# First loads cut into five parts from one row block on, A rows loaded in front of the odd weights, last output stored in three pieces

## The chip, the cores and the metric

The kernel runs on one core of a Trainium2 chip. The metric is the device time of one launch in microseconds (us), and the median of several runs is compared. Lower is better.

## The reference, cut to what matters

Two residual steps on x of shape (128, 64, 1024). The first adds a linear layer with a low-rank adapter chosen per batch element; the second adds a long convolution whose filter is built from a state-space model.

```python
x = x + (einsum('bsd,od->bso', x, W) + bias + einsum('bsr,bor->bso', einsum('bsd,brd->bsr', x, A[ids]), B[ids]))
K = 2 * real(einsum('hn,hnl->hl', Ct, exp(dtA[:, :, None] * arange(1024))))
y = irfft(rfft(x, 2048) * rfft(K, 2048))[..., :1024] + x * D[:, None]
x = x + where(arange(1024) < length, y, 0)
```

Everything is float32. Each product on TensorE is made of three: an operand is split into a rounded part (hi) and what is left (lo), and hi*hi + hi*lo + lo*hi are summed.

## The kernel before, in words

The 128 batch elements are 16 groups of G = 8. One group's x is a tile of NT = 8 row blocks (k = 0 to 7) of 128 rows and N = 512 columns (64 heads by 8 elements). In stage 1 each group goes through the linear layer; output tiles of even number have one set of weights (`w_even`, blocks of `w_pair`) and those of odd number another (`w_odd`, in `v_raw`, `v_hi`, `v_lo`). For most of the work a seven-product scheme with sums of weight blocks is used, but group 0's even tiles are computed plainly: `first_tiles` runs over k, and for each k does QT = 2 output tiles with 3 matmuls each; `plain_tile(2)`, `adapters_down(0)` (x times the A rows), `plain_tile(3)`, `plain_adapters` and the odd products follow. Stage 2 goes over the 64 heads: convolution by blocks, states, and `apply`, which writes the sum into `out_sb` where the mask allows.

All work is ordered by hand, one program per engine, with semaphores between them. SP issues every DMA in the order written. ScalarE (ACT, helper `copy`, L687) writes every hi, VectorE (DVE, `minus_hi`, L1106) every lo, TensorE (PE) multiplies.

At the start SP issues, for `part` 0 to 3, `load_w0(part)` (2 row blocks of first even weights, 256 KB) and `load_x0(part)` (2 row blocks of x, 512 KB), each with a semaphore of its own; after part 0 the adapter ids; then `load_w(0)`, `load_w(1)`, three blocks of odd weights (`load_v`, 512 KB each), a wait for the ids, eight reads of an id into a register (L437), eight A rows (`load_a`, 64 KB each), the bias, eight B rows (`load_b`) and the last block of odd weights.

DVE adds the identity to two diagonal blocks of these weights (`keep_residual`, L1114): this puts the residual x into the product. Part 0 and part 1 have one such block each, and ACT's `split_w0(part)` waits for it. ACT and DVE both go part by part: the weights first, then the two row blocks of x (`split_x`). In `first_tiles` PE waits at every second k for the part's weights (`c_w0lo`) and at every k for `c_xlo`. Until then PE multiplies the identity by itself (`spin`, L1900, SPINS = 14), begun as soon as the identity is there.

After the x parts DVE does `t1(0)`, `split_w(0)`, `keep_residual_22`, `split_w(1)`, the odd weights' `weight_sum_1` (which waits for its three blocks), `split_a(0)`, `weight_sums_3_2`, `split_b(0)`, then `keep_own(0)` and `split_h(0)`, on which `plain_adapters(0)` waits.

At the end, the last head's output is written by two calls of `apply`, one for each half (`par`, a bank of 512 columns), and each half is stored when `c_last` says so:

```python
for par in range(2):
    sp.wait_ge(c_last, par + 1)
    sp.dma_start(out[heads - 1, :, par * BANK:(par + 1) * BANK], ...).then_inc(st_last, 16)
```

## Time and profile before

| what | value |
|---|---|
| median of 3 runs | 1073.74 us (1071.79 to 1074.54) |
| the profiled execution, whole time | 1078.09 us |
| its span in the trace | 1076.4 us |
| TensorE clock granted over the span | 1.00 of full speed (2.4 GHz) |
| PE busy | 1064.2 us (99%) |
| DVE busy | 848.9 us (79%) |
| ACT busy | 716.7 us (67%) |
| DMA queues | 284.62 MB, mean 264 GB/s |

Busy time counts an engine's instructions alone; PE's matmuls overlap and their ends are modelled, so small waits of PE are best read from the starts of its matmuls. A row of the timeline merges instructions of one form that follow each other, with their count, and gives the idle time in front of them and what ended it in brackets.

### The profile page before, as it was taken

Reading aid. Unit: us, or ns where it says so; the run is one execution under the profiler, and the core shown is the slowest. Engines: PE = TensorE matmul, PEld = TensorE weight load, DVE = VectorE, ACT = ScalarE, POOL = GpSimd, SP = SyncE. Lnnn points to the kernel's source line nnn. Section 1 sums busy time; section 2 is a strip of 40 time slices with the busy share of each in tenths; the row PEclk is TensorE's granted clock in tenths of the full one; section 3 lists DMA queues with packets and bytes.
Section 4 is the critical chain, followed back from the end, with each engine's and each line's share of the span. In section 5 each row is a group of like instructions: output and inputs, shape, how many; then the busy total and the mean of one; then the engine's idle time right before and its main releaser. Section 6 shows DMA issues by size and latency. Waiting matters only on the chain.

```text
span 1076.4 us, 21569 instructions
## 1 busy us (share of the span) xinstructions
PE 1064.2 (99%) x8088; PEld 1030.1 (96%) x8088; DVE 848.9 (79%) x1263; ACT 716.7 (67%) x1260; POOL 28.7 (3%) x79
## 2 busy tenths in 40 slices
PE   9999999999999999999999999999999999999998
PEld 8999999999999999999999999999989999999997
DVE  7898886869797696978777696877488888888886
ACT  5755546755747566565647566465498888888885
POOL 0000000000000000000000000000010000000000
PEclk9999999999999999999999999999999999999999
DMA  8586858689786957878785967868798979788873
GB/s 307 193 285 223 273 165 287 199 286 298 243 284 203 289 201 274 245 268 281 228 295 182 302 217 260 284 238 272 251 345 309 337 293 326 305 315 330 287 272 125
DMA packets 162586, 284.62 MB, mean 264 GB/s; under 512 B 10739, under 2 KB 125620, under 8 KB 149044
## 3 DMA queue, kind: packets, MB, share of 16 engines
q1 hardware_dynamic: 162484, 283.26, 76.8%
q8 instruction: 64, 1.05, 0.4%
q14 instruction: 38, 0.31, 0.1%
HBM read 193.96 MB, written 89.26 MB: 263 GB/s over the span
## 4 chain that ended last, share of the span: by engine, by line
PE 59%; SPq 12%; DVE 8%; DMA 8%; ACT 7%; issue 5%; DVEq 0%; ACTq 0%; POOL 0%; POOLq 0%
PE acc L1974 25%; PE acc L1814 16%; PE acc L1820 8%; DMA a_raw<-lora_a 5%; DMA x_scratch<-x_sb 3%; SPq L437 3%; SPq L487 3%; PE acc L2009 3%; DVE x_lo L1106 3%; SPq L441 2%; PE acc L1742 2%; SPq L445 2%; PE acc L1752 2%; PE acc L1786 2%; DVE x_sb L1265 1%
## 5 line engine op out<-in xcount | busy, mean ns | idle before, releaser
L1974 PE MATMUL acc<-u_hi,f_hi 128*128 128x512 f32 (+1 forms) x320 | 128.8, 403 | 0.0
L1814 PE MATMUL acc<-t_hi,v_hi 128*128 128x256 f32 x512 | 123.4, 280 | 5.2 <-ACT x_sb L687 5.2
L1814 PE MATMUL acc<-t_hi,w_pair 128*128 128x256 f32 x960 | 122.6, 280 | 0.8 <-ACT t_hi L687 0.8
L1814 PE MATMUL acc<-t_hi,v_lo 128*128 128x256 f32 x512 | 123.0, 279 | 0.0
L687 ACT ACTIVATE acc<-acc 128x512 f32<-128x512 f32 x93 | 54.0, 580 | 102.9 <-PE acc L1820 102.8
L1974 PE MATMUL acc<-u_lo,f_hi 128*128 128x512 f32 (+1 forms) x320 | 118.3, 370 | 0.0
L1974 PE MATMUL acc<-u_hi,f_lo 128*128 128x512 f32 (+1 forms) x320 | 118.2, 369 | 0.0
L1814 PEld LDWEIGHTS acc<-t_hi,w_pair 128*128 128x128 f32 x960 | 116.8, 188 | 1.2 <-issue 1.1
L1814 PEld LDWEIGHTS acc<-t_hi,v_hi 128*128 128x128 f32 x512 | 96.2, 188 | 6.3 <-ACT x_sb L687 6.3
L1106 DVE TENSOR_TENSOR t_lo<-t_raw,t_hi 128x1024 fp32r<-128x1024 f32 x64 | 78.2, 1222 | 28.0 <-ACT t_hi L687 27.2
L1814 PEld LDWEIGHTS acc<-t_hi,v_lo 128*128 128x128 f32 x512 | 96.2, 188 | 0.0
L1814 PE MATMUL acc<-x_hi,w_pair 128*128 128x256 f32 x720 | 92.9, 281 | 0.5 <-DVE w_pair L1106 0.5
L1814 PE MATMUL acc<-x_hi,v_hi 128*128 128x256 f32 x384 | 92.5, 280 | 0.2 <-ACT acc L687 0.2
L1814 PE MATMUL acc<-x_hi,v_lo 128*128 128x256 f32 x384 | 92.3, 279 | 0.0
L690 ACT ACTIVATE x_sb<-acc,bias_sb 128x256 f32<-128x256 f32 (+1 forms) x128 | 54.6, 482 | 53.9 <-PE acc L1786 52.6
L687 ACT ACTIVATE t_hi<-t_raw 128x1024 fp32r<-128x1024 f32 x64 | 67.7, 1057 | 33.6 <-DVE t_raw L1223 30.3
L1814 PEld LDWEIGHTS acc<-x_hi,w_pair 128*128 128x128 f32 x720 | 87.7, 188 | 1.3 <-issue 0.7
L1664 DVE COPY_PREDICATED out_sb<-mask,acc 128x1024 f32<-128x1024 uint8 (+1 forms) x65 | 84.8, 1306 | 2.4 <-PE acc L1974 2.4
L1106 DVE TENSOR_TENSOR s_lo<-s_raw,s_hi 128x256 fp32r<-128x256 f32 (+1 forms) x128 | 45.1, 353 | 47.9 <-ACT s_hi L687 47.8
L1106 DVE TENSOR_TENSOR x_lo<-x_raw,x_hi 128x512 fp32r<-128x512 f32 x128 | 80.1, 686 | 1.1 <-ACT x_hi L687 0.3
L1106 DVE TENSOR_TENSOR u_lo<-u_raw,u_hi 128x1024 fp32r<-128x1024 f32 (+1 forms) x64 | 77.5, 1211 | 1.3 <-ACT u_hi L687 1.3
L687 ACT ACTIVATE s_raw<-acc 128x128 f32<-128x128 f32 x192 | 51.9, 270 | 32.6 <-PE acc L2009 21.6
(205 smaller groups left out, 2677.2 us busy)
## 6 DMA issues: line engine op xcount, KB each, us to landing
w_pair<-weight_scratch SPq DMA_DIRECT2D x71, 1024.0 KB, 7.9
x_scratch<-x_sb SPq DMA_DIRECT2D x32, 1024.0 KB, 6.6
out<-out_sb SPq DMA_DIRECT2D x63, 512.0 KB, 4.5
x_raw<-x_t SPq DMA_DIRECT2D x15, 2048.0 KB, 12.1
u_raw<-x_scratch SPq DMA_DIRECT2D x14, 2048.0 KB, 11.9
wq_raw<-state_scratch SPq DMA_DIRECT2D x16, 1024.0 KB, 7.7
a_raw<-lora_a SPq DMA_DIRECT2D x128, 64.0 KB, 6.1
b_raw<-lora_b SPq DMA_DIRECT2D x128, 64.0 KB, 2.2
```

The lines of the kernel that those rows point to most:

```text
L437: row = sp.value_load(ids_sb[0:1, b:b + 1], min_val=0, max_val=n_adapters - 1)
L441: sp.dma_start(a_raw[:, i, :, :].rearrange("p t r -> p (t r)"), lora_a[row, :, :].rearrange("a p n -> (a p) n")).then_inc(ld_a, 16)
L445: sp.dma_start(b_raw[i * rank:(i + 1) * rank, :, :].rearrange("p t n -> p (t n)"), lora_b[row, :, :].rearrange("a r n -> (a r) n")).then_i ...
L487: sp.dma_start(r32(w_pair[:, n % 2, :, :, :, :]).rearrange("p s k i n -> p (s k i n)"), ws_d[STREAM.index(j)].rearrange("p s k n -> p (s k ...
L687: return act.activation(dst, src, ACT.Copy)
L690: return act.activation(dst, src, ACT.Identity, bias=bias_sb[:, tile:tile + 1])
L1106: return dve.tensor_tensor(dst, src, r32(hi), ALU.subtract)
L1664: return dve.copy_predicated(out_sb[h % OUT_BUFS][:, pars, :, :].rearrange("p k g n -> p (k g n)"), mask[:, pars, :, :, :].rearrange("p k ...
L1814: pe.matmul(by_row(bank_part(bank, i)), w[:, k, i, :], hi[:, k, :, :], start=opens and i == 0 and k == 0 and s == 0, stop=False, skip_grou ...
L1820: mm = pe.matmul(by_row(bank_part(bank, i)), w_hi[:, k, i, :], lo[:, k, :, :], start=False, stop=False, skip_group_check=True)
L1974: mm = pe.matmul(bank, w, m, start=first and i == 0, stop=last and i == 2, skip_group_check=onto_closed)
L2009: pe.matmul(state_cols(h, i + 1), rot[h % 2][:, :, :].rearrange("p k n -> p (k n)"), s_raw[h % 2][:, :, i, :], start=False, stop=True, ski ...
```

## The change

The first loads are cut at row blocks 1, 2, 4, 6, so into five parts of 1, 1, 2, 2 and 2 row blocks. The first part keeps one semaphore for w and one for x; in each later part w and x share one semaphore, and whoever needs either waits until both have landed (32). The ids are loaded after part 1, not 0. In the first part ACT and DVE split x in front of the weights. The A rows are loaded in front of the three blocks of odd weights, and DVE splits them in front of `weight_sum_1`. The second diagonal block lies in part 2 (row block 2). The last head's second half is written and stored in two pieces.

```diff
     ld_x = sem("ld_x")
-    X0_PARTS = 4
-    ld_x0 = [sem(f"ld_x0_{i}") for i in range(X0_PARTS)]
-    W0_PARTS = 4
-    ld_w0 = [sem(f"ld_w0_{i}") for i in range(W0_PARTS)]
+    FIRST_PARTS = ((0, 1), (1, 2), (2, 4), (4, 6), (6, 8))
+    ld_first_x, ld_first_w = sem("ld_first_x"), sem("ld_first_w")
+    ld_first = [sem(f"ld_first_{i}") for i in range(1, len(FIRST_PARTS))]
     ld_w = [sem(f"ld_w{i}") for i in range(2)]
     ld_ws = [sem(f"ld_ws{i}") for i in range(2)]
...
     EVEN, ODD, BOTH = slice(0, 1), slice(1, 2), slice(0, 2)
+    LAST_PIECES = ((0, slice(0, n_groups)), (1, slice(0, n_groups // 2)), (1, slice(n_groups // 2, n_groups)))
     def u_loaded(q):
...
         return UNIT_PLACES.index((g, place)) if (g, place) in UNIT_PLACES else None
+
+    def first_loaded(part, alone):
+        return alone if part == 0 else ld_first[part - 1]
+
+    def first_rows(part):
+        k0, k1 = FIRST_PARTS[part]
+        return k0 // HALF, k0 % HALF, k0 % HALF + k1 - k0
+
+    def part_of(k):
+        return [k0 <= k < k1 for k0, k1 in FIRST_PARTS].index(True)
     def taps_group(c):
...
             def load_x0(part):
-                w = NT // X0_PARTS
-                sp.dma_start(x_raw[:, part * w:(part + 1) * w, :].rearrange("p t n -> p (t n)"),
-                             x_t[0, :, part * w * N:(part + 1) * w * N]).then_inc(ld_x0[part], 16)
+                k0, k1 = FIRST_PARTS[part]
+                sp.dma_start(x_raw[:, k0:k1, :].rearrange("p t n -> p (t n)"),
+                             x_t[0, :, k0 * N:k1 * N]).then_inc(first_loaded(part, ld_first_x), 16)
             def adapter_of(g, i):
...
             def load_w0(part):
-                c, k = divmod(part * 2, HALF)
+                c, k0, k1 = first_rows(part)
                 w = QT * P
-                sp.dma_start(w_raw[:, c, 1, k:k + 2, :, :].rearrange("p k i n -> p (k i n)"),
-                             w_even[0, c, :, k * w:(k + 2) * w]).then_inc(ld_w0[part], 16)
+                sp.dma_start(w_raw[:, c, 1, k0:k1, :, :].rearrange("p k i n -> p (k i n)"),
+                             w_even[0, c, :, k0 * w:k1 * w]).then_inc(first_loaded(part, ld_first_w), 16)
             def load_w(c):
...
-            for part in range(X0_PARTS):
+            for part in range(len(FIRST_PARTS)):
                 load_w0(part)
                 load_x0(part)
-                if part == 0:
+                if part == 1:
                     sp.dma_start(ids_sb[:, :], ids).then_inc(ld_ids, 16)
             load_w(0)
             load_w(1)
-            load_v(v_raw[:, A11, :, :, :], 0, 0, ld_v11)
-            load_v(v_raw[:, A22, :, :, :], 1, 1, ld_v22)
-            load_v(a21_raw[:, :, :, :], 1, 0, ld_v21)
             sp.wait_ge(ld_ids, 16)
             rows = [adapter_of(0, i) for i in range(G)]
             for i, row in enumerate(rows):
                 load_a(i, row)
+            load_v(v_raw[:, A11, :, :, :], 0, 0, ld_v11)
+            load_v(v_raw[:, A22, :, :, :], 1, 1, ld_v22)
+            load_v(a21_raw[:, :, :, :], 1, 0, ld_v21)
             sp.dma_start(bias_sb[:, :], bias_t).then_inc(ld_bias, 16)
             for i, row in enumerate(rows):
...
                     if q + U_BUFS < quads:
                         load_u(q + U_BUFS)
-            for par in range(2):
-                sp.wait_ge(c_last, par + 1)
-                sp.dma_start(out[heads - 1, :, par * BANK:(par + 1) * BANK],
-                             out_sb[(heads - 1) % OUT_BUFS][:, par, :, :].rearrange("p g n -> p (g n)"))\
+            for i, (par, gs) in enumerate(LAST_PIECES):
+                sp.wait_ge(c_last, i + 1)
+                sp.dma_start(out[heads - 1, :, par * BANK + gs.start * W8:par * BANK + gs.stop * W8],
+                             out_sb[(heads - 1) % OUT_BUFS][:, par, gs, :].rearrange("p g n -> p (g n)"))\
                   .then_inc(st_last, 16)
-            sp.wait_ge(st_last, 32)
+            sp.wait_ge(st_last, 16 * len(LAST_PIECES))
             for i in range(OUT_BUFS):
                 sp.wait_ge(st_out[i], 16 * len(range(i, heads - 1, OUT_BUFS)))
...
             def split_w0(part):
-                act.wait_ge(ld_w0[part], 16)
-                if part < 2:
-                    act.wait_ge(c_wid, part + 2)
-                c, k = divmod(part * 2, HALF)
-                copy(w_pair[:, c, 0, k:k + 2, :, :], w_raw[:, c, 1, k:k + 2, :, :]).then_inc(c_w0hi, 1)
+                if part == 0:
+                    act.wait_ge(ld_first_w, 16)
+                    act.wait_ge(c_wid, 2)
+                else:
+                    act.wait_ge(first_loaded(part, ld_first_w), 32)
+                if part == part_of(2):
+                    act.wait_ge(c_wid, 3)
+                c, k0, k1 = first_rows(part)
+                copy(w_pair[:, c, 0, k0:k1, :, :], w_raw[:, c, 1, k0:k1, :, :]).then_inc(c_w0hi, 1)
             def split_w(c):
...
             def split_x(g, t):
-                if g == 0:
-                    act.wait_ge(ld_x0[t * X0_PARTS // NT], 16)
+                if g == 0 and t == 0:
+                    act.wait_ge(ld_first_x, 16)
+                elif g == 0:
+                    act.wait_ge(first_loaded(part_of(t), ld_first_x), 32)
                 elif t == 0:
                     act.wait_ge(ld_x, 16 * g)
...
             act.wait_ge(c_zero, 1)
             copy(hh[0:heads, 0:1], zeros[:, 0:1])
-            for part in range(W0_PARTS):
+            for part, (k0, k1) in enumerate(FIRST_PARTS):
+                if part == 0:
+                    split_x(0, 0)
                 split_w0(part)
-                for t in range(part * NT // 4, (part + 1) * NT // 4):
+                for t in range(max(k0, 1), k1):
                     split_x(0, t)
             split_w(0)
...
                 return dve.tensor_tensor(ap, ap, ident, ALU.add)
-            def keep_residual(part):
-
-                dve.wait_ge(ld_w0[part], 16)
-                add_identity(w_raw[:, 0, 1, 2 * part, part, :]).then_inc(c_wid, 1)
-                dve.wait_ge(c_wid, part + 2)
+            def keep_residual(i):
+
+                if i == 0:
+                    dve.wait_ge(ld_first_w, 16)
+                else:
+                    dve.wait_ge(first_loaded(part_of(2 * i), ld_first_w), 32)
+                add_identity(w_raw[:, 0, 1, 2 * i, i, :]).then_inc(c_wid, 1)
+                dve.wait_ge(c_wid, i + 2)
             def keep_residual_22():
...
             def split_w0(part):
                 dve.wait_ge(c_w0hi, part + 1)
-                c, k = divmod(part * 2, HALF)
-                ks = slice(k, k + 2)
+                c, k0, k1 = first_rows(part)
+                ks = slice(k0, k1)
                 minus_hi(w_pair[:, c, 1, ks, :, :], w_raw[:, c, 1, ks, :, :], w_pair[:, c, 0, ks, :, :]).then_inc(c_w0lo, 1)
...
             dve.memset(zeros[:, :], 0.0).then_inc(c_zero, 1)
             make_identity()
-            for part in range(W0_PARTS):
-                if part < 2:
-                    keep_residual(part)
+            for part, (k0, k1) in enumerate(FIRST_PARTS):
+                for i in range(QT):
+                    if part == part_of(2 * i):
+                        keep_residual(i)
+                if part == 0:
+                    split_x(0, 0)
                 split_w0(part)
-                for t in range(part * NT // 4, (part + 1) * NT // 4):
+                for t in range(max(k0, 1), k1):
                     split_x(0, t)
             t1(0)
             keep_residual_22()
             split_w(1)
+            split_a(0)
             weight_sum_1()
-            split_a(0)
             weight_sums_3_2()
             split_b(0)
...
                 filter_step(g, 3)
+            def apply_piece(h, par, gs):
+
+                y = acc[:, y_bank(h) + par, gs.start * W8:gs.stop * W8]
+                return dve.copy_predicated(out_sb[h % OUT_BUFS][:, par, gs, :].rearrange("p g n -> p (g n)"),
+                                           mask[:, par, gs, :, :].rearrange("p g t b -> p (g t b)"), y)
+
             def apply(h, pars=slice(0, 2)):
...
             last = heads - 1
             state_low(last, 2, 3)
-            for par in range(2):
+            dve.wait_ge(c_x1c, heads)
+            for par, gs in LAST_PIECES:
                 dve.wait_ge(m_y, last + par + 1)
-                apply(last, slice(par, par + 1)).then_inc(c_last, 1)
+                apply_piece(last, par, gs).then_inc(c_last, 1)
...
             def first_tiles():
                 for k in range(NT):
-                    if k % 2 == 0:
-                        pe.wait_ge(c_w0lo, k // 2 + 1)
+                    if k == FIRST_PARTS[part_of(k)][0]:
+                        pe.wait_ge(c_w0lo, part_of(k) + 1)
                     pe.wait_ge(c_xlo, k + 1)
                     for i in range(QT):
```

## Rows read from the trace of the kernel before

**Rows 1.** The page, its first part: busy us, share and instructions of each engine.

```profile
PE 1064.2 (99%) x8088; PEld 1030.1 (96%) x8088; DVE 848.9 (79%) x1263; ACT 716.7 (67%) x1260; POOL 28.7 (3%) x79
```

**Rows 2.** The timeline of PE and its weight loads: start, us, what, count.

```profile
1.48 5.53 PE L1900 MATMUL acc<-rot 128*128 128x128 f32 x28 [1.48 <-DVE rot L1110]
6.76 0.48 PE L1752 MATMUL acc<-x_hi,w_pair 128*128 128x512 f32 x1
...
9.39 0.89 PE L1752 MATMUL acc<-x_hi,w_pair 128*128 128x512 f32 x2
...
23.51 0.39 PE L1742 MATMUL acc<-x_hi,a_st 128*128 128x256 f32 x1
...
32.86 0.28 PE L1778 MATMUL acc<-hh,b_st 128*128 128x256 f32 x1
...
9.78 0.19 PEld L1752 LDWEIGHTS acc<-x_hi,w_pair 128*128 128x128 f32 x1 [0.42 <-issue]
```

**Rows 3.** The timeline of ACT.

```profile
4.37 0.63 ACT L687 ACTIVATE w_pair<-w_raw 128x512 fp32r<-128x512 f32 x1 [2.06 <-DVE w_raw L1114]
...
8.30 1.16 ACT L687 ACTIVATE x_hi<-x_raw 128x512 fp32r<-128x512 f32 x2 [0.28 <-DMA x_raw<-x_t]
...
21.43 1.16 ACT L687 ACTIVATE a_st<-a_raw 128x512 fp32r<-128x512 f32 x2 [3.17 <-DMA a_raw<-lora_a]
23.60 2.14 ACT L687 ACTIVATE b_st<-b_raw 64x1024 fp32r<-64x1024 f32 x2 [1.01 <-DMA b_raw<-lora_b]
```

**Rows 4.** The timeline of DVE.

```profile
3.98 0.29 DVE L1114 TENSOR_TENSOR w_raw<-w_raw,rot 128x128 f32<-128x128 f32 x1 [2.56 <-DMA w_raw<-w_even]
5.11 0.69 DVE L1106 TENSOR_TENSOR w_pair<-w_raw,w_pair 128x512 fp32r<-128x512 f32 x1 [0.83 <-ACT w_pair L687]
...
8.97 1.29 DVE L1106 TENSOR_TENSOR x_lo<-x_raw,x_hi 128x512 fp32r<-128x512 f32 x2
...
24.63 1.22 DVE L1147 TENSOR_TENSOR v_raw<-v_raw 128x1024 f32<-128x1024 f32 x1
25.88 2.47 DVE L1106 TENSOR_TENSOR b_st<-b_raw,b_st 64x1024 fp32r<-64x1024 f32 x2
28.39 0.68 DVE L1251 TENSOR_TENSOR h_own<-acc,h_own 64x512 f32<-64x512 f32 x1
```

**Rows 5.** The timeline of SP's queue.

```profile
2.49 0.43 SPq L432 DMA_DIRECT2D x_raw<-x_t  x1
...
12.62 3.97 SPq L441 DMA_DIRECT2D a_raw<-lora_a  x8
```

**Rows 6.** DMAs issued at 2.49, 21.5, 21.95, 1073.53: KB each, us to landing.

```profile
x_raw<-x_t SPq DMA_DIRECT2D x1, 512.0 KB, 5.8
...
b_raw<-lora_b SPq DMA_DIRECT2D x2, 64.0 KB, 2.0
...
v_raw<-w_odd SPq DMA_DIRECT2D x1, 512.0 KB, 3.9
...
out<-out_sb SPq DMA_DIRECT2D x1, 256.0 KB, 2.0
```

**Rows 7.** Stretches: busy us by engine, granted clock, DMA share, GB/s.

```profile
5.00:6.00 1.00, 1.00 (x7) 1.00 (x6) 0.89 (x2) 0.90 (x3) 0.00 (x0) 1.00 0.75 231
194.00:196.50 2.50, 1.16 (x9) 1.16 (x10) 1.09 (x3) 2.50 (x7) 0.00 (x0) 1.00 1.00 410
1074.00:1075.00 1.00, 0.00 (x0) 0.00 (x0) 0.00 (x0) 0.00 (x0) 0.00 (x0) 1.00 1.07 416
```

**Rows 8.** The timeline of DVE and SP at the end.

```profile
1072.17 0.73 DVE L1664 COPY_PREDICATED out_sb<-mask,acc 128x512 f32<-128x512 uint8 x1 [0.97 <-PE acc L1974]
...
1072.80 0.70 DVE L1664 COPY_PREDICATED out_sb<-mask,acc 128x512 f32<-128x512 uint8 x1
1072.93 0.33 SPq L676 DMA_DIRECT2D out<-out_sb  x1
...
1073.53 0.33 SPq L676 DMA_DIRECT2D out<-out_sb  x1
```


## The prediction

> **What bounds the kernel now.** The page's first part comes first: PE is busy for 1064.2 of 1076.4 us [rows 1], DVE for 848.9. So a change of loads can be worth only what PE waits at the start, and what stands between its last matmul and the end. The timeline of PE shows the start [rows 2]: the identity products (`spin`) begin at 1.48 and last till about 7.0, the first product of `first_tiles` starts at 6.76, the twelfth (the last of row blocks 0 and 1) at 9.39. Then PE waits once: by its pace the next would start at 9.62, but its weights are loaded at 9.78. The pace is 0.23 us a matmul, from (23.51 - 9.88) / 60, where 9.88 is that weight load and 0.10 more. After this it runs without a gap into `adapters_down` (23.51), `plain_tile(3)` and `plain_adapters` (32.86).
>
> What ended that wait is read from ACT and DVE [rows 3, 4]. ACT starts the hi of x's row block 2 at 8.30, when the DMA lands (issued at 2.49, landed 5.8 us later [rows 5, 6]); DVE's lo runs from 8.97 to about 9.62; PE has it at 9.78. So PE starts row block 2 1.49 us after its x has landed. The weights of that part were ready before: ACT's and DVE's work on them lies in the time in which x was still on its way.
>
> **The first parts.** Part 0 is half as large and x is split first, so its lo values can be there sooner than in the kernel before. It buys nothing: PE comes to `first_tiles` when the spins are over, at 6.76 as now, for nothing in the change starts or shortens them [rows 2]. Row block 1 is needed at 6.76 + 6 * 0.23 = 8.1; its bytes, with part 0's, are those of the old part 0, of which ACT split the weights at 4.37 and DVE at 5.11 [rows 3, 4]. Both are costed at zero, hidden by the spins. If that cover were gone, about 0.6 us could be saved at row block 0 (half of ACT's 0.63 and of DVE's 0.69), but PE would only wait longer at row block 2.
>
> **Row block 2.** Here lies the cost. Its x and w come with part 2, behind the same 1536 KB as before, and now share a semaphore. The identity for the second diagonal block (`keep_residual(1)`) thus waits for x as well, and behind it on DVE stand `split_w0(2)` and the x splits; on ACT `split_w0(2)` waits for both loads and for that identity, and x's hi stands behind it; PE waits for the last of these. From landing L the chain is: 0.05 to start, the identity 0.29, 0.10 to ACT, weights' hi 0.63, 0.11 to DVE (all from the rows at 3.98, 4.37 and 5.11 [rows 3, 4]), weights' lo 0.69, x's lo 0.65 (half of 1.29, with no wait, as its hi was made meanwhile), 0.16 to PE (9.62 to 9.78). Sum 2.68 us, where it was 1.49: 1.19 later.
>
> L itself was 2.49 + 5.8 = 8.29. The bytes ahead of it don't change, so I take 8.3. Bounds: x of part 2 is issued behind two DMAs more, at 0.45 each (0.43 and a gap [rows 5]), so if it keeps its 5.8 us it lands at 9.2 (cost 2.1). The stretch from 5 to 6 us moved 231 GB/s and others 410 [rows 7]; with that dip gone the 180 KB missing come 0.44 us sooner, L = 7.85 (cost 0.75). The rows of the two small parts are half as long, 1 KB for w; what that costs isn't in a row here, and I leave it inside these bounds. Taken: **+1.2 us**, PE idle from 9.62 to about 11.0.
>
> The rules for kernel authors in the Trainium skill's page "DMA: Bandwidth & Descriptors" speak against this part: they ask for 1 MiB or more in a DMA. By the page's fit of a fixed 2.0 us and bytes / 436 GB/s, an estimate, a lone 128 KB load would land 2.3 us after its issue and a 256 KB one 2.6; the trace's comparable time is that of a B row of 64 KB, 2.0 us [rows 6]. By either the small parts would be there long before the spins end, so neither changes the sum.
>
> Parts 3 and 4 have their shared semaphore too. DVE is free of part 2 at about 11.5; part 3 (768 KB more at 410 GB/s: landed at 10.2) then has its weights' lo and x's at 12.8, and PE wants it at 11.0 + 2.7 = 13.7. Part 4, 1.9 later again, is landed at 12.1, ready at 14.9 and wanted at 16.4. Nothing more is lost there. `plain_tile(2)` wants its second weights at about 21.8; DVE, 0.8 later than now, has them at 20.4.
>
> **A rows in front of the odd weights.** In the SP queue the three `load_v` go away from in front of the id reads (1.4 us) and two first loads come in (0.9), so A rows are issued from about 12.1, not 12.62 [rows 5], till 16.0. They no longer stand behind 1.5 MB: last issue 15.6 plus 2.0 to 5.0 gives 17.6 to 20.6, where ACT waited 3.17 us for them until 21.43 [rows 3]. But PE did not wait: `adapters_down` starts at 23.51 on its pace, and will be wanted at 24.7. Worth zero now; it would be worth something only to a PE that came sooner. What it costs is behind it: the odd weights are issued at 16.1 to 17.5 and everything after them in the queue (bias, B rows, the fourth odd block) 0.9 later. A lone 512 KB took 3.9 us [rows 6], further ones 1.3 each: the third lands at about 22.6. DVE then has three sums of 1.22 (22.7 to 26.3) and two lo of B of 1.22 (to 28.7) [rows 4]; B lands at 22.4 + 2.0 = 24.4 (ACT took it at 23.60). `keep_own` can begin at 28.7, where it now begins at 28.39. PE, 1.2 late, gives it its input at 29.6. So there are 0.9 us of cover and the cost is zero. With no delay of PE it would be 0.3; if the odd weights landed 2 us later than that, 1.1 on top of what is forecast.
>
> All that follows hangs on PE or on this DVE chain, both later by about the same; PE has no long wait to absorb it, as its 99% says [rows 1].
>
> **The end.** DVE copies the first half at 1072.17 (0.73) and the second at 1072.80 (0.70); the stores are issued at 1072.93 and 1073.53 [rows 8], and the second lands after 2.0 us [rows 6]. In three pieces the first is unchanged. A half copy costs about 0.4 (512 columns take 0.70), so the second store is issued at 1073.3 and the third, held by the queue's 0.37 per issue, at 1073.67: 0.14 after the old second. The DMA engines are saturated from 1074 to 1075 (share 1.07, 416 GB/s [rows 7]), so pieces that come sooner wait behind the first 256 KB and the last byte leaves when it did. Bounds: -0.2 (landing shrinks with a store of 128 KB: 0.33 less 0.14) to +0.3 (short rows are slower). Taken: **+0.1**.
>
> **Sum.** 1.2 + 0.1 = +1.3 us. Made on the profiled execution (1078.09 whole, 1076.4 span), which is 4.35 above the median of the runs; the difference is carried over to the median: 1073.74 + 1.3 = 1075.0.
>
> **Rivals.**
> 1. The loads come sooner and the wait shrinks. To break even at row block 2, L must be 7.1, 1.2 sooner; the most that can be had is the present wait, 0.26. Then about -0.2, 1073.5. For it: the dip to 231 GB/s. Against: the same bytes. 10%.
> 2. Landing is set by the issue, not by the bytes: L = 9.2, cost 2.1, with the end 1076.0. For it: the 5.8 us are longer than 512 KB needs; against: by the rates in [rows 7] the queue was full. 20%.
> 3. TensorE's clock falls. PE would idle 1.4 us just after its start. In the stretch from 194.0 to 196.5 PE was idle for 1.34 us and the granted clock stayed at 1.00, 2.4 GHz [rows 7]. Were it 1.2 GHz for a stretch after the wait, half of the stretch would be lost; with 1.3 already gone, 4 us of it make the kernel slower by over 0.3% (3.2 us), and over all 8.2 us of the rest of `first_tiles`, which would take 16.4, it is 1083.2. 4%. The Trainium skill, "TensorE: Matmul & The Clock Gate", its HAM clock gate part, has PE drop to half clock after idling; the stretch above bears no such drop out.
> 4. The odd weights or B come much later than reckoned, and DVE's chain sets `plain_adapters`: +2.4, 1076.1. 6%.
>
> The forecast itself has 60%, with 1074.3 to 1076.1 as its own range (cost 0.75 to 2.1, end -0.2 to +0.3). The medians of either kernel move too (the three runs span 2.8 us), so the range is 1072.5 to 1077.5. Within 0.3%, about what this measurement can tell from no change, lie the forecast and rivals 1, 2 and 4: 93%, less a little for both tails. Faster by more would need 3.2 us, and PE waits for less than that at the start: 2%. Slower: 5%, rival 3 and an unforeseen wait.
>
> **What would show it.** In the changed kernel's profile: spins and first product at 1.48 and 6.76 as before; one gap of PE at row block 2, its matmuls from about 11.0; in front of it on DVE the order identity, w lo, x lo, with the identity waiting for x's DMA at about 8.3; `adapters_down` at about 24.7 with A rows split by 21.7; `keep_own` at about 29.6; the last store issued 0.14 later after the last matmul. Wrong would be: row block 2 before 10, a wait of PE at `plain_adapters`, a clock below 1.00, or an end above 1077.5.

## The result

The changed kernel's median is 1076.49 us (1073.64 to 1079.22, 22 runs) against 1073.15 us for the kernel before (1071.31 to 1075.28, 22 runs beside it). The ratio is 1.0029, 95% interval 1.0021 to 1.0037: 3.1 us slower by the ratio, 3.3 by the medians. That is just inside the 0.3% that the prediction took as no change, and the loss is real, since the interval excludes 1. Forecast was +1.3 us. The predicted range of 1072.5 to 1077.5 held the time, but 2 us of the loss were not in the sum. The forecast's own narrower range (1074.3 to 1076.1) did not hold it. The wide one did with some luck: it starts from 1073.74, the median of three runs, and the median of 22 is 0.6 lower.

The profiled execution of the changed kernel took 1075.75 us, with a span of 1074.0. This is less than the 1078.09 of the kernel before, so spans of single executions say nothing here; the two are compared by the starts of the same work. What stands behind the first product of the odd tiles is the same work in all kernels but for the last stores, and in the 14 profiles it took from 1037.4 us (changed kernel) to 1043.0 us (experiment 2). So a profile shows where the start loses time, but a loss read there agrees with a median only to within that scatter. The page, first part (as [rows 1]):

```profile
PE 1063.2 (99%) x8088; PEld 1030.0 (96%) x8088; DVE 848.7 (79%) x1265; ACT 716.5 (67%) x1261; POOL 28.6 (3%) x79
```

The timeline of PE and its weight loads, changed kernel (start us, us, what, count, idle time before and what ended it); L1783 is `first_tiles`, L1773 `adapters_down`, L1809 `plain_adapters`, L1845 the first product of the odd tiles:

```profile
1.48 5.97 PE L1931 MATMUL acc<-rot 128*128 128x128 f32 x28 [1.48 <-DVE rot L1128]
7.20 0.48 PE L1783 MATMUL acc<-x_hi,w_pair 128*128 128x512 f32 x1
...
9.81 0.39 PE L1783 MATMUL acc<-x_hi,w_pair 128*128 128x512 f32 x1
11.86 0.47 PE L1783 MATMUL acc<-x_hi,w_pair 128*128 128x512 f32 x1 [1.66 <-DVE x_lo L1124]
...
35.39 0.36 PE L1809 MATMUL acc<-hh,b_st 128*128 128x256 f32 x1 [0.45 <-issue]
...
36.57 0.36 PE L1845 MATMUL acc<-x_hi,v_hi 128*128 128x256 f32 x1
...
11.82 0.19 PEld L1783 LDWEIGHTS acc<-x_hi,w_pair 128*128 128x128 f32 x1 [2.05 <-DVE w_pair L1124]
```

There are two losses here, not one. At row block 2 the weight load starts at 11.82 where it was 9.78 [rows 2]: 2.04 late. At `plain_adapters` it is 35.39 for 32.86 [rows 2]: 2.53 late, with a new wait of 0.45 in front of it. The first product of the odd tiles starts at 36.57; in the kernel before its row is:

```profile
33.83 0.36 PE L1814 MATMUL acc<-x_hi,v_hi 128*128 128x256 f32 x1
```

So PE is 2.74 late from there on.

The timeline of ACT, changed kernel: the weights of row block 2, then `split_b(0)` and the copy of PE's result that `keep_own` needs.

```profile
9.68 0.63 ACT L697 ACTIVATE w_pair<-w_raw 128x512 fp32r<-128x512 f32 x1 [3.01 <-DVE w_raw L1132]
...
26.44 2.15 ACT L697 ACTIVATE b_st<-b_raw 64x1024 fp32r<-64x1024 f32 x2 [5.70 <-DMA b_raw<-lora_b]
...
29.70 0.60 ACT L697 ACTIVATE h_own<-acc 64x512 f32<-64x512 f32 x1
```

The timeline of DVE, changed kernel:

```profile
9.29 0.29 DVE L1132 TENSOR_TENSOR w_raw<-w_raw,rot 128x128 f32<-128x128 f32 x1 [1.88 <-DMA x_raw<-x_t]
10.41 0.69 DVE L1124 TENSOR_TENSOR w_pair<-w_raw,w_pair 128x512 fp32r<-128x512 f32 x1 [0.83 <-ACT w_pair L697]
11.02 1.29 DVE L1124 TENSOR_TENSOR x_lo<-x_raw,x_hi 128x512 fp32r<-128x512 f32 x2
...
24.85 1.23 DVE L1168 TENSOR_TENSOR v_raw<-a_raw,v_raw 128x1024 f32<-128x1024 f32 x1 [1.70 <-DMA a_raw<-w_odd]
...
28.63 2.47 DVE L1124 TENSOR_TENSOR b_st<-b_raw,b_st 64x1024 fp32r<-64x1024 f32 x2
31.13 0.68 DVE L1272 TENSOR_TENSOR h_own<-acc,h_own 64x512 f32<-64x512 f32 x1
```

The first three rows are the predicted chain behind x's landing; the fourth is the new wait, for the third odd block. `keep_own` is 2.74 late (31.13 for 28.39 [rows 4]) though ACT had its input ready at 30.30. SP's queue, changed kernel:

```profile
3.44 0.43 SPq L442 DMA_DIRECT2D x_raw<-x_t  x1
...
12.49 3.97 SPq L451 DMA_DIRECT2D a_raw<-lora_a  x8
16.50 0.91 SPq L501 DMA_DIRECT2D v_raw<-w_odd  x2
17.45 0.43 SPq L501 DMA_DIRECT2D a_raw<-w_odd  x1
```

DMAs issued at 3.44 and at 17.45, changed kernel (KB, us to landing):

```profile
x_raw<-x_t SPq DMA_DIRECT2D x1, 512.0 KB, 5.8
...
a_raw<-w_odd SPq DMA_DIRECT2D x1, 512.0 KB, 7.3
```

Stretches of the changed kernel (busy us by engine, granted clock, DMA share, GB/s):

```profile
11.00:12.00 1.00, 0.14 (x1) 0.18 (x2) 1.00 (x3) 1.00 (x3) 0.00 (x0) 1.00 1.08 438
...
20.00:22.00 2.00, 2.00 (x11) 1.65 (x10) 2.00 (x3) 0.74 (x2) 0.00 (x0) 1.00 0.99 386
22.00:24.00 2.00, 2.00 (x11) 1.65 (x10) 1.12 (x5) 0.00 (x0) 0.00 (x0) 1.00 0.92 227
24.00:26.00 2.00, 2.00 (x12) 1.73 (x11) 1.15 (x1) 0.00 (x0) 0.00 (x0) 1.00 0.88 203
```

The last two rows matter most: while the third odd block, the bias and the B rows are in the queue together, the DMA engines are busy for 0.9 of the time and move half of what they moved at 11 us. At the end of the kernel:

```profile
1070.04 0.34 PE L2005 MATMUL acc<-s_hi,f_lo 128*128 128x384 f32 x1
...
1070.71 1.31 SPq L686 DMA_DIRECT2D out<-out_sb  x3
```

From the start of the last matmul to the end of the span are 3.96 us; before it was 1076.4 less 1072.32, so 4.08 by the span as the profile rounds it.

### The profile page after: what moved, and what is told of

It reads as the page before. It is cut to its first block, busy times and chain, and to the rows that moved or that the text cites. A ratio compares the mean times of both kernels' runs of the same rounds, so it can differ in the third digit from the quotient of the medians.

```text
span 1074.0 us, 21574 instructions
## 1 busy us (share of the span) xinstructions
PE 1063.2 (99%) x8088; PEld 1030.0 (96%) x8088; DVE 848.7 (79%) x1265; ACT 716.5 (67%) x1261; POOL 28.6 (3%) x79
## 4 chain that ended last, share of the span: by engine, by line
PE 86%; DVE 4%; ACT 3%; SPq 2%; DMA 2%; issue 2%; DVEq 0%; ACTq 0%
PE acc L1845 32%; PE acc L2005 25%; PE acc L1851 16%; PE acc L1773 5%; PE acc L1817 4%; PE acc L2040 3%; PE acc L1783 2%; DMA a_raw<-lora_a 1%; DVE x_lo L1124 1%; SPq L447 1%; DMA x_raw<-x_t 1%; SPq L451 1%; ACT L874 0%; DMA x_scratch<-x_sb 0%; ACT t_hi L697 0%
## 5 line engine op out<-in xcount | busy, mean ns | idle before, releaser
L1845 PE MATMUL acc<-t_hi,v_hi 128*128 128x256 f32 x512 | 123.2, 280 | 2.8 <-ACT x_sb L697 2.8
L1845 PE MATMUL acc<-t_hi,v_lo 128*128 128x256 f32 x512 | 123.0, 279 | 0.0
L1845 PE MATMUL acc<-t_hi,w_pair 128*128 128x256 f32 x960 | 122.5, 280 | 0.1
L1845 PEld LDWEIGHTS acc<-t_hi,w_pair 128*128 128x128 f32 x960 | 116.9, 188 | 0.3 <-issue 0.3
L1845 PEld LDWEIGHTS acc<-t_hi,v_hi 128*128 128x128 f32 x512 | 96.2, 188 | 3.3 <-ACT x_sb L697 3.2
L1845 PEld LDWEIGHTS acc<-t_hi,v_lo 128*128 128x128 f32 x512 | 96.2, 188 | 0.0
L1845 PE MATMUL acc<-x_hi,w_pair 128*128 128x256 f32 x720 | 92.8, 281 | 0.5 <-DVE w_pair L1124 0.5
L1845 PE MATMUL acc<-x_hi,v_hi 128*128 128x256 f32 x384 | 92.5, 280 | 0.2 <-ACT acc L697 0.2
L1845 PE MATMUL acc<-x_hi,v_lo 128*128 128x256 f32 x384 | 92.3, 279 | 0.0
L1845 PEld LDWEIGHTS acc<-x_hi,w_pair 128*128 128x128 f32 x720 | 87.7, 188 | 1.2 <-issue 0.7
L1694 DVE COPY_PREDICATED out_sb<-mask,acc 128x1024 f32<-128x1024 uint8 x63 | 83.2, 1320 | 1.4 <-PE acc L2005 1.4
L697 ACT ACTIVATE s_raw<-acc 128x128 f32<-128x128 f32 x192 | 51.9, 270 | 32.5 <-PE acc L2040 21.5
```

The costliest lines, as they stand in the source:

```text
L697: return act.activation(dst, src, ACT.Copy)
L1694: return dve.copy_predicated(out_sb[h % OUT_BUFS][:, pars, :, :].rearrange("p k g n -> p (k g n)"), mask[:, pars, :, :, :].rearrange("p k ...
L1845: pe.matmul(by_row(bank_part(bank, i)), w[:, k, i, :], hi[:, k, :, :], start=opens and i == 0 and k == 0 and s == 0, stop=False, skip_grou ...
```

## The experiments

Two theories were set against each other; the granted clock came in as a third after the first four kernels. Theory 1: all of the loss is the wait at row block 2 (x issued later, and identity and weights now waiting for x). Theory 2: the chain of odd weights and B rows on DVE sets the loss. Ratios are to the kernel before, run beside it on the same chip (experiments 1 to 4 on one chip, 5 to 8 on a second, 9 to 12 on a third); medians of different chips are not compared. "PE resumes" is row block 2's first matmul, "odd" the start of DVE's first sum of odd weights, "B" the start of ACT's `split_b(0)`, "p1" the first product of the odd tiles, each from the one profiled execution. Where PE did not wait, its start at row block 2 is given as "no wait".

| kernel | PE resumes | odd | B | p1 | ratio, 95% interval |
|---|---|---|---|---|---|
| before | 9.88 | 20.55 | 23.60 | 33.83 | 1 |
| changed | 11.86 | 24.85 | 26.44 | 36.57 | 1.0029 (1.0021 to 1.0037) |
| changed again | 11.97 | 25.00 | 27.35 | 36.74 | 1.0041 (1.0027 to 1.0055) |
| A rows back | 11.62 | 21.90 | 25.69 | 36.89 | 1.0048 (1.0031 to 1.0065) |
| A rows back, again | 12.00 | 22.35 | 25.62 | 38.69 | 1.0020 (1.0011 to 1.0028) |
| part 2 unshared | 10.87 | 24.46 | 26.89 | 36.28 | 1.0033 (1.0021 to 1.0046) |
| both | 11.58 | 22.48 | 25.08 | 35.46 | 1.0014 (1.0002 to 1.0026) |
| before, A rows moved | no wait | 25.22 | 26.87 | 36.94 | 1.0019 (1.0008 to 1.0030) |
| before, three pieces | 10.55 | 21.00 | 24.31 | 34.39 | 0.9997 (0.9985 to 1.0009) |
| before, shared | 10.8 | 21.24 | 23.87 | 34.59 | 1.0003 (0.9993 to 1.0014) |
| before, ids later | 10.50 | 21.11 | 23.79 | 34.39 | 1.0002 (0.9989 to 1.0015) |
| before, row block 2 alone | no wait | 20.18 | 24.61 | 34.01 | 0.9993 (0.9984 to 1.0002) |
| changed, B rows wait | 12.28 | 23.62 | 29.50 | 38.89 | one run |
| changed, spins in the gap | 12.14 | 26.60 | 29.30 | 38.68 | 1.0032 (1.0018 to 1.0045) |

### A rows back behind the odd weights (1)

```diff
+            load_v(v_raw[:, A11, :, :, :], 0, 0, ld_v11)
+            load_v(v_raw[:, A22, :, :, :], 1, 1, ld_v22)
+            load_v(a21_raw[:, :, :, :], 1, 0, ld_v21)
             sp.wait_ge(ld_ids, 16)
...
                 load_a(i, row)
-            load_v(v_raw[:, A11, :, :, :], 0, 0, ld_v11)
-            load_v(v_raw[:, A22, :, :, :], 1, 1, ld_v22)
-            load_v(a21_raw[:, :, :, :], 1, 0, ld_v21)
...
+            weight_sum_1()
             split_a(0)
-            weight_sum_1()
```

> Two theories of the 2.74 us by which the changed kernel's first odd product (p1 of group 0) starts later, 36.57 instead of 33.83. Theory 1, row block 2: its x lands 0.9 later and its weights wait for it, so PE resumes at 11.86 instead of 9.81, 2.05 later, and the rest is small change. Theory 2, the chain of odd weights and B rows: moved behind the A rows they land so late that DVE reaches keep_own at 31.13, 2.74 later, and this alone would set p1, wherever PE is. With A rows back behind the odd weights, row block 2 is untouched: PE resumes at about 11.8 by both. p1 by both theories at 35.9 (2.05 late), the loss of the whole run 2.0 to 2.1 us over the kernel before; keep_own at about 30.3, given by PE and not by DVE. If p1 stays at 36.5, theory 2 is wrong.

Ratio 1.0048, 6 runs: 5.2 us slower by the medians, where 2.0 to 2.1 were expected. The B chain no longer counts: `keep_own` (31.39) waits 2.03 for ACT's copy of PE's result. Yet p1 is at 36.89. The reason is in the stretches of this kernel (clock is the column before the DMA share):

```profile
10.00:11.00 1.00, 0.00 (x0) 0.00 (x0) 0.82 (x2) 1.00 (x3) 0.00 (x0) 1.00 1.00 379
11.00:12.00 1.00, 0.38 (x1) 0.41 (x2) 1.00 (x3) 0.97 (x3) 0.00 (x0) 0.60 1.07 428
12.00:13.00 1.00, 1.00 (x3) 0.75 (x3) 1.00 (x3) 0.82 (x2) 0.00 (x0) 0.50 1.02 410
13.00:14.00 1.00, 1.00 (x4) 0.77 (x3) 0.94 (x3) 0.72 (x2) 0.00 (x0) 0.50 1.01 414
14.00:15.00 1.00, 1.00 (x5) 0.81 (x4) 1.00 (x2) 1.00 (x3) 0.00 (x0) 0.69 1.05 430
```

```profile
8.80 0.39 PE L1783 MATMUL acc<-x_hi,w_pair 128*128 128x512 f32 x1
11.62 0.77 PE L1783 MATMUL acc<-x_hi,w_pair 128*128 128x512 f32 x1 [2.43 <-DVE x_lo L1124]
```

In this execution the spins were over early (first product at 6.17), so PE waited 2.43 us at row block 2 instead of 1.66, and then TensorE ran at 1.2 GHz, 0.50 of its clock, for about 3 us. That is the predicted rival 3, and it explains the p1 of this execution. It does not explain the ratio: this execution, at 1077.80 us, was the fastest of the six, and the two runs with a mean granted clock of 1.000 took 1079.58 and 1082.63. Where the rest of the 5.2 us went is not known.

### Part 2's w and x on semaphores of their own (2)

```diff
+    ld_x2 = sem("ld_x2")
...
+        if part == 2 and alone is ld_first_x:
+            return ld_x2
...
-                    act.wait_ge(first_loaded(part, ld_first_w), 32)
+                    act.wait_ge(first_loaded(part, ld_first_w), both(part))
```

`both(part)` is 16 for part 2 and 32 for the others.

> The changed kernel with w and x of part 2 (row blocks 2 and 3) on a semaphore each. x still lands at about 9.2, but its weights are ready before: PE resumes 1.5 us after landing, at about 10.75 instead of 11.86. Theory 1 (row block 2 alone sets the loss): p1 comes 1.1 sooner, at 35.5, and the run is 1.1 us faster than the changed kernel. Theory 2 (odd weights and B rows set it): keep_own stays at 31.1 and p1 at 36.5, the run is not faster, and PE waits about 1.5 us in front of plain_adapters instead of 0.45.

Ratio 1.0033, 12 runs: no gain over the changed kernel's 1.0029 that shows. PE resumes a whole microsecond sooner, and loses it again:

```profile
10.87 0.47 PE L1789 MATMUL acc<-x_hi,w_pair 128*128 128x512 f32 x1 [0.63 <-DVE x_lo L1130]
...
35.10 0.36 PE L1815 MATMUL acc<-hh,b_st 128*128 128x256 f32 x1 [1.13 <-DVE hl L1130]
```

The wait before `plain_adapters` has grown from 0.45 to 1.13; the third odd block is still summed only at 24.46. p1 comes 0.3 sooner than in the changed kernel, not 1.1. Theory 1 alone falls here: with its wait shortened, the other chain takes over.

### Both together (3)

The edits of the two experiments above in one kernel.

> The changed kernel with A rows back and part 2 on two semaphores. What is left is the late landing of x's row block 2 (two more DMAs issued in front of it). Both theories: PE resumes at about 10.75 and p1 comes at about 34.8, 1.0 after the kernel before; the run is 0.9 to 1.0 us slower than it.

Ratio 1.0014 (12 runs), p1 at 35.46: the best of the three, though 34.8 was expected. `keep_own` starts at 29.97, and PE does not wait in front of `plain_adapters` (34.52). In this execution x of row block 2 was on chip only at 10.08 (it is still issued two DMAs later than in the kernel before, but in experiment 2, with the same order, it was there by 9.4), and PE resumed at 11.58; the rest of the loss lies there in this profile.

### The kernel before with nothing but the A rows moved (4)

```diff
-            load_v(v_raw[:, A11, :, :, :], 0, 0, ld_v11)
-            load_v(v_raw[:, A22, :, :, :], 1, 1, ld_v22)
-            load_v(a21_raw[:, :, :, :], 1, 0, ld_v21)
             sp.wait_ge(ld_ids, 16)
...
+            load_v(v_raw[:, A11, :, :, :], 0, 0, ld_v11)
+            load_v(v_raw[:, A22, :, :, :], 1, 1, ld_v22)
+            load_v(a21_raw[:, :, :, :], 1, 0, ld_v21)
```

and `split_a(0)` ahead of `weight_sum_1()` on DVE.

> The kernel before with only the A rows moved in front of the odd weights (and their split on DVE). PE is not late at row block 2 (9.8). Theory 1: nothing is lost, p1 at 33.8 to 34.1. Theory 2: the odd weights (third block issued at about 16.1 instead of 7.3) and the B rows behind them collide, the third block lands at 23 to 24, keep_own comes at about 30.3, p1 at 35.5 to 36, and the run is 1.7 to 2.2 us slower than the kernel before.

Ratio 1.0019 (1.0008 to 1.0030), 12 runs: 2.0 us, of 1.7 to 2.2 expected. This settles that the step costed at zero is not free. The timeline of DVE and of PE, this kernel:

```profile
25.22 1.23 DVE L1147 TENSOR_TENSOR v_raw<-a_raw,v_raw 128x1024 f32<-128x1024 f32 x1 [3.69 <-DMA a_raw<-w_odd]
```

```profile
35.75 0.36 PE L1778 MATMUL acc<-hh,b_st 128*128 128x256 f32 x1 [2.65 <-DVE hl L1106]
...
36.94 0.36 PE L1814 MATMUL acc<-x_hi,v_hi 128*128 128x256 f32 x1
```

PE did not wait at row block 2 at all here, reached `adapters_down` at 23.73, and stood 2.65 us in front of `plain_adapters`. The third odd block, issued at 16.73, took 8.4 us to land. After that wait the clock fell here too, to 0.70, 0.50, 0.50 and 0.60 in the four stretches from 37 to 41, of which the first two:

```profile
37.00:38.00 1.00, 1.00 (x7) 1.00 (x8) 0.96 (x2) 1.00 (x3) 0.00 (x0) 0.70 0.25 53
38.00:39.00 1.00, 1.00 (x6) 1.00 (x6) 1.00 (x1) 0.71 (x1) 0.00 (x0) 0.50 0.10 21
```

This execution was the slowest of the twelve (1081.03 us), so its p1, 3.1 late, is more than the median lost.

### The last output in three pieces, alone (5)

The kernel before with `LAST_PIECES` and `apply_piece` as in the diff of the change.

> The kernel before with only the last output in three pieces. From the start of the last matmul to the end of the span it was 4.04 us before and 3.96 in the changed kernel. Expected 3.9 to 4.1 and no difference in time that shows; if the third store cost what the prediction took (0.1 to 0.3), 4.1 to 4.3.

Ratio 0.9997 (0.9985 to 1.0009), 12 runs: nothing. Its start is the kernel before's, yet x of row block 2 was taken at 9.05, not 8.30 [rows 3], and PE resumed at 10.55. So the landing moves by some 0.7 us between executions of one order of loads, and with it p1: 34.39 here for 33.83.

### Shared semaphores in the kernel before (6)

```diff
-                             x_t[0, :, part * w * N:(part + 1) * w * N]).then_inc(ld_x0[part], 16)
+                             x_t[0, :, part * w * N:(part + 1) * w * N]).then_inc(ld_w0[part], 16)
...
-                act.wait_ge(ld_w0[part], 16)
+                act.wait_ge(ld_w0[part], 32)
```

The waits in `split_x` and `keep_residual` are changed in the same way.

> The kernel before (four parts of two row blocks) with one semaphore for w and x of each part. Order and size of the loads are as before, so x's row block 2 lands at about 8.3, and PE resumes 2.6 us later, at about 10.9 (9.8 before). p1 at about 34.9. This is the cost of the shared wait by itself as the prediction reckoned it: 1.1 us.

Ratio 1.0003 (0.9993 to 1.0014), 12 runs. Part 0 now waits for both loads as well, so the first product comes at 7.83, after a wait of 1.34 for x's lo. PE needs row block 2 later by that, and the wait in front of it is short: its weights are loaded at 10.73. x of row block 2 had landed at 8.1 (issued at 2.49, 5.6 us), so the identity starts here:

```profile
8.20 0.28 DVE L1114 TENSOR_TENSOR w_raw<-w_raw,rot 128x128 f32<-128x128 f32 x1
```

From landing to PE are 2.6 us, as reckoned (2.6), where it was 1.49 before. In the kernel before x landed nearly as early (8.29): against it PE resumes 0.95 later and p1 is 0.76 later (34.59 for 33.83). Against experiments 5 and 8 p1 is only 0.2 later, but there x was taken at 9.05 and 9.00. So by the traces a shared semaphore costs 0.8 to 0.95 us at an equal landing, somewhat less than the 1.1 expected; the interval of the ratio, 0.8 us faster to 1.5 us slower, can neither confirm nor exclude it.

### Ids behind part 1 (8)

The kernel before with `if part == 1:` instead of `if part == 0:` ahead of the load of the ids, which puts part 1's w and x one DMA earlier.

> The kernel before with only the load of the ids moved behind part 1, so the loads of part 1 are issued 0.36 us sooner. x of part 1 landed 5.8 us after its issue in both kernels (2.49 and 3.44). If its landing is set by its issue, it now lands at about 7.9 and PE resumes at 9.6 to 9.7, with no wait at row block 2; if it is set by the bytes in front of it, it stays at 8.3 and PE at 9.8. The time of the run can't show 0.2 us.

Ratio 1.0002 (0.9989 to 1.0015), 12 runs. x of row block 2 was taken at 9.00, later than either 7.9 (set by the issue) or 8.3 (set by the bytes). The spread that experiment 5 showed is larger than the 0.4 us in question, so whether issue or bytes set the landing is not told by single profiles.

### B rows held back until the third odd block has landed (7)

```diff
             load_v(a21_raw[:, :, :, :], 1, 0, ld_v21)
+            sp.wait_ge(ld_v21, 16)
             sp.dma_start(bias_sb[:, :], bias_t).then_inc(ld_bias, 16)
```

> The changed kernel with bias and B rows issued only once the third odd block has landed. In the changed kernel that block needed 7.3 us from issue to landing, where the one in front of it needed 4.4. If B rows that come behind it slow it down, it now lands 5.0 to 5.7 us after its issue, at about 22.7 to 23.2; if it is slow by itself, it stays at 7.3. B rows land at about 29.5 by either, so the run is slower.

One run. The third odd block landed in 5.6 us instead of 7.3. Its landing and two of the stretches shown for the changed kernel:

```profile
a_raw<-w_odd SPq DMA_DIRECT2D x1, 512.0 KB, 5.6
```

```profile
20.00:22.00 2.00, 2.00 (x11) 1.65 (x10) 1.78 (x3) 1.16 (x3) 0.00 (x0) 1.00 0.99 401
22.00:24.00 2.00, 2.00 (x11) 1.65 (x10) 1.93 (x7) 0.00 (x0) 0.00 (x0) 1.00 0.09 31
```

With nothing behind them the odd blocks were over by about 23, where the changed kernel still moved 203 to 227 GB/s until 26. So the delay comes, at least in part, from what shares the queue with the block. The margin is smaller than 7.3 to 5.6 suggests: in the five other profiles of kernels with A rows in front the block took 7.3, 7.5 and 7.9 (changed kernel, experiments 9 and 12), 8.4 (experiment 4), but only 6.6 in experiment 2. And the edit holds back the bias (4 KB, issued first) and all later loads with the B rows, so which of them slows the block is not shown. As a remedy it fails, since B rows then come at 29.50 and p1 at 38.89; part of that is the clock, which was 0.50 from 13 to 16 here after a wait of 2.54 at row block 2.

### The changed kernel again, and A rows back again (9, 10)

> The changed kernel once more, unchanged, beside the next three on one chip. Expected 0.25 to 0.35% slower than the kernel before, PE resuming at row block 2 at 11.6 to 12.3, and about half of its runs with a mean granted clock of 0.998 or less, of the kernel before none.

> The changed kernel with A rows back behind the odd weights, a second time. The first time it had a median 0.48% above the kernel before (six runs), more than the whole change, while its p1 would be at 35.4 without the clock's fall. Theory 2 (odd weights and B rows) wants it no slower than the changed kernel beside it, by about 0.05%. If it is slower again, there is a cost in it that neither theory has.

The changed kernel gave 1.0041 (7 runs; 1.0025 to 1.0035 was expected), with 6 of the 7 low in clock and 1 of the 27 of the kernel before. A rows back gave 1.0020 (11 runs), and 1.0048 in experiment 1 on another chip. The two intervals of the same kernel do not overlap (1.0031 to 1.0065, 1.0011 to 1.0028). So the interval from one chip understates what a ratio does from chip to chip, and differences of 0.1 to 0.2% between these kernels are not settled by it. Side by side on this chip the kernel with A rows back is 2.6 us faster than the changed kernel by the medians, which is what theory 2 allows, and more than the 0.05% that it reckoned. The profiled execution of A rows back shows the clock again, here for a longer stretch:

```profile
11.00:18.00 7.00, 6.00 (x14) 4.77 (x15) 6.87 (x11) 4.67 (x8) 0.00 (x0) 0.52 1.03 414
18.00:19.00 1.00, 1.00 (x5) 0.76 (x5) 0.96 (x3) 0.01 (x1) 0.00 (x0) 0.97 1.04 359
```

PE had waited 2.94 us (from its product at 8.67 to 12.00), and `adapters_down` came at 28.54, where the changed kernel, with PE resuming 0.14 sooner, had it at 25.57. That execution took 1081.19 us, the slowest of the eleven; the median of the eight runs of this kernel whose mean clock was 1.000 is 1077.8.

### Row block 2's x loaded by itself (11)

```diff
+                pieces = ((2, 3, st_last), (3, 4, ld_x0[1])) if part == 1 else ((part * w, (part + 1) * w, ld_x0[part]),)
+                for k0, k1, landed in pieces:
...
-                    act.wait_ge(ld_x0[t * X0_PARTS // NT], 16)
+                    act.wait_ge(st_last if t == 2 else ld_x0[t * X0_PARTS // NT], 16)
```

The kernel before, with only x of row block 2 (256 KB) cut off from the load that PE waits for.

> A version that may beat both: the kernel before, with x of part 1 loaded as two row blocks, so that row block 2 needn't wait for row block 3's 256 KB (0.65 us at 400 GB/s). Expected: PE resumes at row block 2 0.5 to 0.7 us sooner than the 9.8 to 10.5 of the kernels that start as the kernel before does, so at 9.6 to 9.9, with almost no wait; p1 at 33.8 to 34.0; the run 0.3 to 0.6 us faster than the kernel before, which is at the limit of what can be told.

Ratio 0.9993 (0.9984 to 1.0002), 11 runs. x of row block 2 was taken at 7.86, and there is no wait; the matmuls go through row block 2 at their pace:

```profile
9.21 0.62 PE L1754 MATMUL acc<-x_hi,w_pair 128*128 128x512 f32 x2
9.67 0.39 PE L1754 MATMUL acc<-x_lo,w_pair 128*128 128x512 f32 x1
9.89 0.62 PE L1754 MATMUL acc<-x_hi,w_pair 128*128 128x512 f32 x2
```

It has the lowest ratio of all kernels run, and is not to be told from the kernel before. That the cut took the wait away is not shown by this profile: the first product came at 7.30 here, so PE wanted row block 2 only at about 10.1, and experiment 4, with the old loads and a first product at 7.09, had no wait either.

### Spins in the gap (12)

```diff
                 for k in range(NT):
+                    if k == 2:
+                        spin(8)
```

The changed kernel, with 16 identity products more to be multiplied while PE waits.

> The changed kernel with eight identity products more (about 1.9 us of PE) in front of the wait at row block 2, so that PE isn't idle there. If the fall of the clock after this wait is what half of the changed kernel's runs lose, mean clocks of 0.998 or less go away and the median is 0.5 to 0.7 us below the changed kernel's beside it; p1 stays at 36.5, for DVE sets it. If the clock costs nothing here, the two medians are the same.

Ratio 1.0032 (1.0018 to 1.0045), 9 runs, against 1.0041 of the changed kernel beside it. The timeline of PE, this kernel:

```profile
9.68 1.95 PE L1933 MATMUL acc<-rot 128*128 128x128 f32 x16
12.14 0.47 PE L1783 MATMUL acc<-x_hi,w_pair 128*128 128x512 f32 x1 [0.51 <-DVE x_lo L1124]
...
37.50 0.36 PE L1811 MATMUL acc<-hh,b_st 128*128 128x256 f32 x1 [2.31 <-DVE hl L1124]
```

The gap is filled and the clock stays at 1.00 after it. Of the 9 runs 2 had a mean clock of 0.998 or less, where the unchanged copy beside it had 6 of 7. The number of runs is small, and the gain in the time (1.7 us by the medians, 0.5 to 0.7 expected) lies inside the intervals. In this execution the B rows came at 29.30, so the DVE chain made PE wait 2.31 at `plain_adapters`; spins do nothing for that one.

## Why the prediction was right, and where it was wrong

**First parts.** As predicted: the spins cover them. The first product started at 7.20, not 6.76, but that is the spins' own length (see below).

**Row block 2, +1.2 forecast, 2.04 measured: the term was mis-sized.** The chain was right: identity waiting for x's DMA at 9.29, weights' lo at 10.41, x's lo at 11.02, PE's weight load at 11.82. From landing (3.44 + 5.8 = 9.24) that is 2.58, forecast 2.68. The size failed at "The bytes ahead of it don't change, so I take 8.3". L was 9.24, the other bound, 5.8 us after its later issue: rival 2's time to 0.04. That is not proof of its mechanism, since the old start gave 8.3 to 9.05 (the kernel before, experiments 5 and 8), PE then resuming at 9.88 to 10.55; against these the changed kernel is 1.3 to 2.0 late at row block 2, not 2.04 in every execution. The other half of the term, the longer chain behind the landing, is borne out by experiment 2 (PE resumes a microsecond sooner with the semaphores apart) and experiment 6 (2.6 us from landing to PE with shared ones).

**A rows, zero forecast: this is the step that failed.** "The third lands at about 22.6 ... So there are 0.9 us of cover and the cost is zero." It landed at 24.75 (17.45 + 7.3), and B's rows were taken at 26.44, not 24.4. The reckoning gave a lone load 3.9 us and each further one 1.3, as if nothing else followed in the queue; in the changed order the bias and eight B rows follow at once and the block needs 7.3 (6.6 to 8.4 in the other profiles with A rows in front, 5.6 with all that follows held back). The 3.9 us were not those of a lone load either: the fourth odd block was issued at 21.95 right behind the B rows, and a store of 1 MB followed it at 22.99 (timeline of SP, kernel before). So it is not that anything follows, but what. DVE's chain then ends 2.4 later than reckoned, at 31.1, and `keep_own` starts 2.74 late, 0.8 after PE's result was ready for it. The prediction had this as rival 4, "the odd weights or B come much later than reckoned, and DVE's chain sets `plain_adapters`", with 6%; that is what happened, on top of rival 2. Experiment 4 shows it alone (1.0019), experiment 2 shows that it hides what is gained at row block 2, experiment 3 that with both undone p1 is at 35.46 instead of 36.57 and the ratio 1.0014, the lowest of the four kernels on that chip.

**How the two add up.** They run side by side and the later one counts: 2.04 at row block 2, 2.74 at `keep_own` and p1. So of the 1.5 us that p1 lost beyond the forecast of 1.2, about 0.8 come from the landing of x and 0.7 from DVE's chain. That is why undoing one alone moved p1 so little.

**The clock, rival 3, 4% forecast.** Of the 22 runs of the changed kernel 10 had a mean granted clock of 1.000 (median 1075.91), 12 had 0.997 or 0.998 (median about 1077.1); of the kernel before, 1 of its 85 runs beside the experiments was that low. The first group lies 2.76 above the median of before; the traces give 2.74 for p1, or 2.2 if the p1 of 34.39 of experiments 5 and 8 stands for the old start. The second group is another 1.2 later, and 12 of 22 runs of it make the mean some 0.65 later: 2.2 to 2.74 and 0.65 are 2.9 to 3.4, for the measured 3.3. That the sum fits so well is partly luck, since the same work behind p1 took 1037.4 to 1043.0 us in single executions, and in experiments 1 and 2 the runs low in clock were hardly slower by their medians (0.1 and 0.15 us) than those at 1.000. (A mean of 0.999 tells nothing: in the profiles of experiments 3, 8 and 12, with that mean, the clock fell only after the last matmul.) In the profiles that show the drop while PE works (experiments 1, 4, 7, 10) there is a wait of PE of 2.4 to 2.9 us beside it. In experiments 1 and 10 the clock falls before the wait is over (0.60 and 0.61 in the stretch from 11 to 12), in experiment 4 the wait ends at 35.75, the clock is 1.00 from 36 to 37 and falls in the stretch from 37 to 38. The prediction had argued from an idle time of 1.34 us that kept its clock [rows 7], the part of a wait of 1.47 that lies in that stretch; the wait of 1.66 in the profiled execution of the changed kernel kept it too, and so did experiment 12, whose gap was filled. That the low runs of the changed kernel itself lost their clock at row block 2 is argued from these, not shown: the executions profiled of it, one on each of two chips, held 1.00.

**The end, +0.1 forecast.** 3.96 us for 4.08, and 0.9997 (0.9985 to 1.0009) alone: nothing.

**What stays open.** Whether issue or bytes set the landing of x; whether bias or B rows slow the third odd block; why the same kernel's ratio was 1.0048 on one chip and 1.0020 on another.

## What to carry to other kernels

Where a load is moved, give the loads moved back the time that they take with what now follows them in the queue, not that of a lone load; look for the chain on another engine that they feed, and compute its end as carefully as the bottleneck engine's. When two chains meet at one instruction, price both and take the later, and expect that undoing one of them shows little. A wait of TensorE costs its length, and where it grows from one and a half to two and a half microseconds, possibly also the clock of the stretch after it; keep row blocks that start the kernel on loads issued early, and semaphores apart where a short step waits for the weights alone.

## What the runs showed of the hardware

- 512 KB with 4 KB of bias and eight 64 KB rows behind it in the queue took 7.3 us to land (7.5, 7.9 and 6.6 in experiments 9, 12 and 2, 8.4 in experiment 4); with these held back 5.6 (experiment 7, one run). In the changed kernel the DMA engines were busy for 0.88 to 0.92 of the time at 203 to 227 GB/s, where they moved 386 GB/s at a share of 0.99 in the two microseconds before: the busy share alone does not tell the bytes moved.
- With waits of 2.43, 2.54, 2.65 and 2.94 us (experiments 1, 7, 4, 10) TensorE was granted 1.2 GHz for 3 to 7 us; matmuls of 512 columns then came 0.42 us apart (12.56 to 12.98 in experiment 10) instead of 0.23. Waits of 1.47 us (kernel before), 1.66 (changed kernel) and 2.31 (experiment 12) were not followed by it. Length alone does not decide: after the last matmul of the kernel before, the clock was 1.00 for the 3.4 us from 1073 to the end of the span with PE idle.
- The 28 spins took 4.76 us (experiment 1) to 6.32 us (experiment 3), with the granted clock shown as 1.00 in both. The first product of the kernel thus starts up to 1.4 us sooner or later (6.03 in experiment 10, 7.47 in experiment 3), in kernels that do not differ there; where the spins end early and the load is late, PE's wait is longer by that. The difference lies in the pace: in experiment 1 PE had 7 of them in each stretch of a microsecond from 2 to 4, then 9 and 12, in experiment 3 only 6 or 7 up to the end, and the 16 spins in the gap of experiment 12 took 1.95 us. The pace changes as if the clock rose at some point, but the column of the granted clock does not show it; the cause stays open.
